# A fused attention, selective-scan and quantised-FFN kernel: silu groups moved to ScalarE, a fourth of eight products by C moved to VectorE, and a reordered front

## The reference

```
h = tok(x)                                   # patches, 12-head attention
h = concat([h, txt], axis=1)
h = h + mixer(layernorm(h))
h = h + ffn(layernorm(h))

mixer:  xi, res = split(x @ W_in)            # 384 channels each
        u = silu(causal_conv4(xi) + conv_b)
        delta, B, C = split(u @ W_x, [48, 64])
        delta = softplus(delta @ W_dt + b_dt)
        a = exp(cumulated later delta * A)   # A = -exp(A_log), 384 x 16
        xs = cumsum(delta*u*B * a) / (a + 1e-12)
        y = sum over the 16 states of xs * C, plus u * D
        return (y * silu(res)) @ W_out
ffn:    bitlinear (ternary weights, 8-bit activations), silu(gate)*up, bitlinear
```

## Time and profile before

| | before |
|---|---|
| runs, median | 541.2 us (537.76 to 542.29) |
| profiled execution, its own time | 541.64 us |
| its span | 539.8 us |
| front, up to the first scan | 139.8 us |
| first scan to the end of the last guarded states | 139.8 to 503.7 us |
| tail | 503.7 to 539.8 us |
| mean granted TensorE clock | 0.855 |

### The profile page before, as it was taken

One profiled execution on the slowest core, in us unless ns is written; L12 is line 12 of the kernel. 1 busy time (PEld: TensorE's weight loads), 2 busy tenths in 40 slices (PEclk: granted clock), 3 DMA queues, 4 the chain that ended last, 5 costly groups with the idle time before them and its releaser, 6 DMA issues.

```text
span 539.8 us, 5082 instructions
## 1 busy us (share of the span) xinstructions
PE 397.8 (74%) x1484; PEld 222.7 (41%) x1484; DVE 399.8 (74%) x481; ACT 338.3 (63%) x601; POOL 367.3 (68%) x288
## 2 busy tenths in 40 slices
PE   5929999686896585899677599875656686665753
PEld 1303677353553242565343356542323352332523
DVE  3024255622589899989999988989999989879544
ACT  1102544413967876777779857996886786796253
POOL 3002563002878988979998998998789999969401
PEclk9968999968798887999678889998987887778865
DMA  8390000005600003710000470000056100000000
GB/s 314 83 205 10 1 2 0 2 0 185 286 0 5 1 1 128 279 60 4 0 1 17 159 273 21 4 22 0 0 177 231 60 2 22 1 1 0 0 23 22
DMA packets 11547, 35.10 MB, mean 65 GB/s; under 512 B 2320, under 2 KB 6208, under 8 KB 11296
## 3 DMA queue, kind: packets, MB, share of 16 engines
q1 hardware_dynamic: 11120, 33.99, 18.7%
q10 hardware_dynamic: 400, 0.79, 0.4%
HBM read 33.40 MB, written 1.38 MB: 64 GB/s over the span
## 4 chain that ended last, share of the span: by engine, by line
POOL 31%; DVE 11%; PE 9%; issue 9%; ACT 6%; DVEq 0%; ACTq 0%; POOLq 0%
POOL big L465 15%; POOL big L471 10%; DVE PS L1305 5%; PE PS L817 4%; PE PS L593 3%; POOL big L509 2%; ACT PS L1001 2%; DVE big L1314 1%; PE PS L743 1%; DVE big L1320 1%; POOL big L447 1%; DVE big L1399 1%; ACT big L1053 1%; ACT big L1010 1%; PE PS L797 1%
## 5 line engine op out<-in xcount | busy, mean ns | idle before, releaser
L817 PE MATMUL PS<-big,eighth 128*128 128x384 f32 x384 | 170.9, 583 | 74.3 <-POOL big L471 73.2
L1305 DVE TENSOR_TENSOR_SCAN PS<-PS,big 128x768 f32<-128x768 f32 x96 | 168.6, 1756 | 18.5 <-ACT PS L1001 16.2
L465 POOL TENSOR_TENSOR big<-big,bc 128x768 f32<-128x768 f32 x96 | 175.1, 1839 | 0.0
L817 PEld LDWEIGHTS PS<-big,eighth 128*128 128x128 f32 x384 | 81.9, 224 | 144.8 <-POOL big L471 93.6
L471 POOL TENSOR_TENSOR big<-big,bc 128x768 f32<-128x768 f32 x60 | 109.5, 1824 | 37.3 <-DVE big L1314 37.1
L1001 ACT ACTIVATE PS<-big,Aneg 128x384 f32<-128x384 f32 x192 | 103.7, 572 | 39.6 <-DVE big L1320 25.4
L1010 ACT ACTIVATE big<-big,guard,Ahalf 128x380 f32<-128x380 f32 x192 | 122.5, 690 | 0.0
L1314 DVE SCALAR_TENSOR_TENSOR big<-big,PS 128x768 f32<-128x768 f32 x60 | 57.0, 951 | 5.8 <-ACT big L1010 0.5
L430 POOL TENSOR_TENSOR big<-bc,cst_sb 96x1536 f32<-96x1536 f32 x8 | 22.0, 2753 | 56.2 <-ACT bc L911 45.9
L593 PE MATMUL PS<-big,w_in_sb 96*128 96x384 f32 x96 | 42.9, 586 | 5.5 <-DVE big L1266 5.0
L593 PE MATMUL PS<-big 128*64 128x34 f32 (+3 forms) x400 | 43.8, 287 | 0.0
(11 more groups left out here) (152 smaller groups left out, 486.8 us busy)
## 6 DMA issues: line engine op xcount, KB each, us to landing
bc<-bc_rows SPq DMA_DIRECT2D x32, 768.0 KB, 4.4
bc<-in_x_cols_dram SPq DMA_DIRECT2D x3, 512.0 KB, 6.5
bc<-in_x_cols_dram SPq DMA_DIRECT2D x1, 1536.0 KB, 8.7
out_dram<-h SPq DMA_DIRECT2D x4, 288.0 KB, 2.3
big<-in_f_in_dram SPq DMA_DIRECT2D x1, 768.0 KB, 18.0
bc<-in_cw_dram ACTq DMA_DIRECT2D x1, 576.0 KB, 5.7
h<-in_bo_dram SPq DMA_DIRECT2D x3, 192.0 KB, 15.1
w_in_sb<-in_w_in_dram SPq DMA_DIRECT2D x1, 576.0 KB, 13.0
```

The lines of the kernel that those rows point to most:

```text
L465: P.tensor_tensor(pair(vR[:, g % VRING]), part(du, q, m).unsqueeze(1).broadcast_to([128, PAIR, QT]), rows_of(g, 0), ALU.mult).then_inc(sem ...
L817: ins = pe.matmul(y_sum, eighth[:, :], vR[:, g % VRING, QT * e:QT * (e + 1)], start=False, stop=True, skip_group_check=True)
L1305: V.tensor_tensor_scan(h_, h_, vR[:, g % VRING], 0.0, ALU.mult, ALU.add).then_inc(sem("scan_done"), 1)
```

## The change

Four things are changed together.

1. Silu of u and z becomes one ACT instruction from PSUM each, three in a row (`su`, `sz`), two steps or more after the matmuls they read. The DVE multiplications go. The factor 2 and the halves that made up for it go too.
2. DVE multiplies by C at four of eight pairs in place of three; in group 3 at pairs 1, 3, 4 and 7.
3. The preparation of group 1 no longer has six steps ahead of step 0; all of it stands beside steps 0 to 21. Small ACT instructions on a spare tile (`warm`) are put in so that a table is loaded ahead of its first use: softplus, Exp, and Silu in the tail.
4. The two FFN weight loads stand ahead of the nine loads of the bias and the text. Each group's output is stored in two parts.

```diff
-VECTOR_C = (1, 4, 6)
+VECTOR_C = ((1, 3, 4, 6), (1, 3, 4, 6), (1, 3, 4, 6), (1, 3, 4, 7))
...
-             cv0=-26, cv1=-25, cv2=-24, tu0=-25, tu1=-24, tu2=-23, us0=-24, us1=-23, us2=-22, x=-21, x_out=-20,
-             dt0=-19, dt1=-19, dt2=-19, sp=-18, times_u=-16, later0=-14, later1=-11, later2=-9, edges=-6,
-             z0=-16, z1=-15, z2=-14, tz0=-15, tz1=-14, tz2=-13, zs0=-14, zs1=-13, zs2=-12)
+             cv0=-26, cv1=-25, cv2=-24, su=-22, x=-18, x_out=-17,
+             dt0=-16, dt1=-16, dt2=-16, sp=-15, times_u=-13, later0=-14, later1=-12, later2=-9, edges=-6,
+             z0=-14, z1=-13, z2=-13, sz=-11)
...
-FIRST_MIXER = dict(stats=-6, root=-6, xn=-5, turn=-5, turned=-4, xi0=-3, xi1=-2, xi2=-2, tap0=0, tap1=0, tap2=1,
-                   cv0=1, cv1=2, cv2=2, tu0=2, tu1=3, tu2=3, us0=4, us1=5, us2=5, x=6, x_out=7, dt0=8, dt1=8, dt2=8, sp=9,
-                   times_u=11, later0=12, later1=14, later2=17, edges=19, z0=12, z1=13, z2=14, tz0=13, tz1=14, tz2=15,
-                   zs0=14, zs1=15, zs2=16)
+FIRST_MIXER = dict(stats=0, root=1, xn=2, turn=2, turned=3, xi0=3, xi1=4, xi2=4, tap0=4, tap1=5, tap2=5,
+                   cv0=5, cv1=6, cv2=6, su=8, x=13, x_out=14, dt0=15, dt1=15, dt2=15, sp=16,
+                   times_u=18, later0=17, later1=18, later2=19, edges=21, z0=11, z1=12, z2=12, sz=14)
...
-FIRST_STEP, LAST_STEP = -6, STEPS + 33
+FIRST_STEP, LAST_STEP = 0, STEPS + 33
...
-SCALAR_WORK = dict(xn=3, turned=2, tap0=1, tap1=1, tap2=1, tu0=1, tu1=1, tu2=1, tz0=1, tz1=1, tz2=1, x_out=1, sp=6,
+SCALAR_WORK = dict(xn=3, turned=2, tap0=1, tap1=1, tap2=1, su=5, sz=5, x_out=1, sp=6,
...
+            load("ffn", f_in_raw, f_in.rearrange("p m n -> p (m n)"))
+            load("ffn", f_out_raw, f_out.rearrange("p m n -> p (m n)"))
...
-            load("ffn", f_in_raw, f_in.rearrange("p m n -> p (m n)"))
-            load("ffn", f_out_raw, f_out.rearrange("p m n -> p (m n)"))
...
-            def store(q):
-                sp.wait_ge(sem("left_f2"), ORDINAL["f2", q, 1])
-                sp.dma_start(out[QB * q:QB * (q + 1)].rearrange("b l d -> (b l) d").rearrange("(i p) d -> p i d", p=128),
-                             tiles(q)).then_inc(sem("out_stored"), 16)
+            def store(q, j):
+                sp.wait_ge(sem("left_f2"), ORDINAL["f2", q, j])
+                t = slice(2, 3) if j else slice(0, 2)
+                sp.dma_start(out[QB * q:QB * (q + 1)].rearrange("b l d -> (b l) d").rearrange("(i p) d -> p i d", p=128)[:, t],
+                             tiles(q, t)).then_inc(sem("out_stored"), 16)
...
-            def tanh_z(q, j):
+            def silu_z(q, j):
...
-                A.activation(part(sres, q, j), job_bank("z", q, j)[:, 0:QT], ACT.Tanh, scale=0.5).then_inc(sem("tz_ready"), 1)
-            def tanh_first():
+                A.activation(part(sres, q, j), job_bank("z", q, j)[:, 0:QT], ACT.Silu).then_inc(sem("left_z"), 1)
+            def silu_u(q, j):
+                job_here(act, "cv", q, j)
+                if q >= 2:
+                    act.wait_ge(sem("y_acc"), QSTEPS * (q - 2) + BLOCK * j + 1)
+                    act.wait_ge(sem("du_ready"), delta_of(q - 2, j))
+                A.activation(part(u, q, j), job_bank("cv", q, j)[:, 0:QT], ACT.Silu).then_inc(sem("left_cv"), 1)
+            def silu_first():
...
-                A.activation(part(du, 0), part(u, 0), ACT.Tanh, scale=0.5).then_inc(sem("tu_first"), 1)
+                A.activation(part(u, 0), part(u, 0), ACT.Silu).then_inc(sem("u_first"), 1)
...
-                A.activation(xdbc[:, :], job_bank("x", q, 0)[0:F, 0:QT], ACT.Identity, scale=0.5).then_inc(sem("left_x"), 1)
+                A.activation(xdbc[:, :], job_bank("x", q, 0)[0:F, 0:QT], ACT.Copy).then_inc(sem("left_x"), 1)
...
-                for j in range(CT):
-                    for q in due("tu%d" % j, g):
-                        tanh_u(q, j)
-                for j in range(CT):
-                    for q in due("tz%d" % j, g):
-                        tanh_z(q, j)
+                for q in due("su", g):
+                    for j in range(CT):
+                        silu_u(q, j)
+                for q in due("sz", g):
+                    for j in range(CT):
+                        silu_z(q, j)
...
+                for q in due("center", g):
+                    if q == LAST:
+                        A.activation(warm[:, 2:3], v128[:, 0:1], ACT.Silu)
...
                 if i == 8:
-                    tanh_first()
+                    silu_first()
+                    silu_z(0, 0)
+                    silu_z(0, 1)
                 p = i - 1
...
                 if i == 9:
+                    A.activation(warm[:, 0:1], v128[:, 0:1], ACT.Softplus)
                     x_out(0)
...
                     first_tap(0, 2)
-                    tanh_z(0, 0)
                 if i == 8:
-                    tanh_z(0, 1)
-                    tanh_z(0, 2)
+                    silu_z(0, 2)
             for m in range(CT):
                 softplus(0, m)
+            A.activation(warm[:, 1:2], v128[:, 0:1], ACT.Exp)
             for g in range(FIRST_STEP, 0):
...
-                V.tensor_scalar(diagD[:, m, :], ident, dpar[:, m:m + 1], 0.25, ALU.mult, ALU.mult)
-            V.tensor_scalar(eighth[:, :], ident, 0.125, None, ALU.mult)
+                V.tensor_scalar(diagD[:, m, :], ident, dpar[:, m:m + 1], None, ALU.mult)
+            V.tensor_scalar(half_eye[:, :], ident, 0.5, None, ALU.mult)
...
-            def silu_z(q, j):
-                job_here(dve, "z", q, j)
-                dve.wait_ge(sem("tz_ready"), CT * q + j + 1)
-                V.scalar_tensor_tensor(part(sres, q, j), part(sres, q, j), 1.0, job_bank("z", q, j)[:, 0:QT],
-                                       ALU.add, ALU.mult).then_inc(sem("left_z"), 1)
-            def silu_first():
...
                     conv(0, 2)
-                    silu_z(0, 0)
-                if i == 8:
-                    silu_first()
-                    silu_z(0, 1)
-                    silu_z(0, 2)
             V.memset(gR.rearrange("p s (r l) -> p (s r) l", l=L)[:, :, L - 1:L], 1.0).then_inc(sem("edges_set"), 1)
```

More of the change, by code:

```diff
@@ L119 @@
 for i in range(NTL):
-    LAST_READ.update({"xi%d" % i: "tap%d" % i, "cv%d" % i: "us%d" % i, "z%d" % i: "zs%d" % i, "dt%d" % i: "sp", "out%d" % i: "add%d" % i,
+    LAST_READ.update({"xi%d" % i: "tap%d" % i, "cv%d" % i: "su", "z%d" % i: "sz", "dt%d" % i: "sp", "out%d" % i: "add%d" % i,
                       "gate%d" % i: "silu", "up%d" % i: "times%d" % i})
@@ L400, in _ @@
                 if q >= 2:
-                    store(q - 2)
-            store(2)
-            store(3)
-            sp.wait_ge(sem("out_stored"), 16 * NQ)
+                    store(q - 2, 0)
+                    store(q - 2, 1)
+            for q in range(NQ - 2, NQ):
+                store(q, 0)
+                store(q, 1)
+            sp.wait_ge(sem("out_stored"), 32 * NQ)
         @block.gpsimd
@@ L816, in sum_y @@
                 for e in range(PAIR):
[L817 removed]
+                    ins = pe.matmul(y_sum, half_eye[:, :], vR[:, g % VRING, QT * e:QT * (e + 1)], start=False, stop=True,
                                     skip_group_check=True)
@@ L1429, in after @@
                         gate(q, m)
-                for j in range(CT):
-                    for q in due("us%d" % j, g):
-                        silu_u(q, j)
-                for j in range(CT):
-                    for q in due("zs%d" % j, g):
-                        silu_z(q, j)
                 for j in range(2):
```

17 lines of the change are left out of this document (3 added, 14 removed).

## The result

The change makes the kernel faster: 517.76 us median of four runs (515.52 to 523.06) against 540.92 of the kernel before on the same chip, ratio 0.959 with a 95% interval of 0.951 to 0.968. The forecast was 516, range 507 to 527.

What follows compares the result with a forecast made beforehand. No engine full over the whole span; DVE 93% full in the steps, POOL close behind. From 541.64: loads -12.8, front's end -8.4, DVE's work +3.0, DVE's waits -5.3, tail -1.9, giving 516.2 us; 80% range 507 to 527.

Steps and rivals of the forecast that it cites:

- Loads, -12.8: Front: FFN weights land sooner, PE's 10.7 us wait and 2.1 us of half clock go; -12.8 us, bounds -9.3 and -12.8.
- The rival that the weights don't land sooner: Front: the images, not small pieces, hold the queue, so the 12.8 us is not gained; 529 us, chance 0.07.
- End of the front, -8.4: Front's end: projection's wait, softplus table and group 1's preparation no longer delay the first scan; -8.4 us, bounds -5 and -8.4.
- DVE's work, +3.0: Steps: 12 products by C add 11.5 us, norm statistics 1.2; z and u multiplications drop 4.9 and 4.8; net +3.0.
- DVE's waits, -5.3: Steps: DVE's waits become 11.2 us in place of 16.5, six new ACT blocks costing 1.0 each; -5.3 us.
- Tail, -1.9: Tail: the last product by C leaves POOL, so the tail begins 1.9 us sooner for PE; -1.9 us.
- What would show it: Expected trace signs: gapless PE, first scan near 118.5, DVE over 94%, POOL under 87%, ACT waits about 11 us.
- three marks against me: Wrong if scans behind new blocks wait over 2.5 us, first scan passes 122, or DVE's POOL/PE waits exceed 4 us.
- Expensive blocks: Steps: each new ACT block costs DVE the worst-case 2.48 us; 525 us, chance 0.15.
- DVE bound to the full: Steps: ACT's blocks hide and DVE waits only where it did for ACT; 507 us, chance 0.10.
- ACT becomes the bound: Steps: each of six blocks is exposed whole, 30.6 us in all, and the old 16.5 stay; 552 us, chance 0.03.
- A switch that stops ACT twice as long: Steps: a table switch stops ACT 2.56 us, a block takes 6.6 us; 532 us, chance 0.03.

Runs made afterwards that it cites:

- second profile: The changed kernel run again with no edit and profiled anew: span 517.1 us, profiled execution 518.9 us, median 517.98 us, ratio 0.958.
- silu as before: Kernel before with the change's loads, front order, tables ahead and four-of-eight products, but single Tanh and DVE multiplications kept, projection at step 10: 519.32 us, 0.965.
- first profile: The changed kernel's original profiled execution, the slowest of its four runs: 523.06 us, span 521.3 us.
- two more moves: Changed kernel, group 1's z behind its projection, group 3's at step 69, group 2's at 28 to 31, group 1's convolutions spread: 510.42 us, 0.941.
- four of eight alone: Kernel before with one edit, DVE multiplying by C at four of eight pairs: 538.69 us, ratio 0.997.
- run without switches: Changed kernel with Tanh in place of Silu in the six blocks of groups 1 to 3, so no table switch: 508.72 us, 0.947.

## Why the prediction was right, and which of its steps were not

The sum was 516.2; the second profile has 518.9, the median is 517.8. By the stretches of the table (the last product by C, 0.96 us, lies behind the last scan) it foresaw -21.2 in the front, -3.3 in the steps and -0.9 in the tail. Measured on the second profile: -23.1, +1.7, -1.4. Errors of 1.9 and 5.0 us of opposite sign met in the sum, so the time was nearer than its parts: that much of the hit is luck.

- *Loads, -12.8.* Right in mechanism and a little small: 14.4 us to the first scan. The wait of 10.7 went whole and the half clock did not come back, which gave 2.3 (16.80 us in place of 19.13), put at 2.1. Another 0.6 is that PE was through with the patch embedding at 29.16 in place of 29.80, which lies within the spread told below as open; the last 0.8 was not traced. The rival that the weights don't land sooner is out.
- *End of the front, -8.4.* 8.7 (125.4 to 116.7). The 2.2 of the projection's wait is right: 2.25 us, gone here and back in silu as before. But the wait ended with the multiplication of z, which the bank hung on, and not with that of u, and the projection behind it ran at a granted clock of 0.58 there, 3.60 us in place of 2.10. These 1.5 us the working did not have. The rest came with the order of group 1's preparation, by the rows alone: no run put that order back. That the table ahead gains nothing of its own stood in the working (the third softplus waits for PE), and the run without it shows it.
- *DVE's work, +3.0.* +2.6 up to the last scan, where 2.0 of the 3.0 were due. The terms were not all there: the running sums, which I took as constant, moved with POOL.
- *DVE's waits, -5.3.* This is the step that failed. Idle fell by 0.9 (26.7 to 25.7), or not at all in the first profile. By the terms, in the second profile:
  - The waits for POOL, 2.3, for PE's FFN output, 2.0, and for Tanh, 0.7, went as counted.
  - The 2.8 for PE's sums, put down to POOL's lag and counted as gone, stayed at 2.9. Of the old ones 0.6 was left at step 25, but the moved convolutions of group 1 brought a new one of 2.3 at step 9 (it goes in two more moves, where they are spread).
  - Of the 8.7 on ACT's account 1.1 stayed, away from the new blocks, where I had left 5.2. I laid this to Tanh's place next to the convolution; four of eight alone took 4.4 off with Tanh where it was, so that reason is not shown.
  - The six new blocks, put at 1.0 each, are the term that missed most: DVE's waits behind the three of z were 3.5, 3.4 and 4.6 us (3.8, 3.4 and 4.6 in the first profile), and nearly nothing behind the three of u. That is 11.5 in all against 6.0. The run without switches gives the same from the other side, 10.9 us of idle.

  So errors of +2.9, -4.1 and +5.5 make up nearly all of the 4.4 us by which the step was off. The average of the nine old waits was no measure, since a block costs by what stands next to it: z of groups 2 and 3 has the FFN's block two steps on, z of group 1 a bank that PE hands over. I had named both places and allowed under 3 us for the bank; the stop was 2.79 and the scan's wait 3.81.
- *Tail, -1.9.* -1.4 by the stretch, where -0.9 was due, once the projection has the same clock. In the profiled execution PE's half clock in the output projection took 2.6 us of it back; nothing in the working allowed for that.
- *What would show it* (numbers of the first profile). PE without a gap, at full clock: yes. First scan near 118.5: 116.2. POOL under 87%: 84% (306.85 of 364.34). DVE over 94%: no, 92.6% (337.34). Waits on ACT about 11: 13.0 without the one ahead of the first scan. Waits on POOL gone: yes, and those on PE 3.6, under the 4 that I had set. Of the three marks against me one was met: two scans behind new blocks waited over 2.5 us, 3.81 and 2.73.
- *Rivals.* "Expensive blocks" came half true: its two places are where the waits are, and their 11.8 us (first profile) lie between the 6.0 of the forecast and its 14.9. "DVE bound to the full", 507, did not come; the run without switches, 508.7, shows about what it would have given. "ACT becomes the bound" is out: it had 30.6 us of new waits. A switch that stops ACT twice as long is out: in the rows above Silu follows its load by 0.01 us, and decays follow theirs by as little. The Trainium skill's drain of about 1380 ns per switch, "ScalarE: Activation LUTs", section "What ACT_TABLE_LOAD costs", does not show in this kernel; its 1283 ns do.

What stays open: the first scan of kernels with the same front lay between 114.4 and 116.7. Most of this is there when PE comes to the product of the sums, at 28.5 in the soonest of them and 30.2 in the latest; from there to the first scan it is 85.9 to 86.5 us in all. Why the patch embedding ahead of it ends sooner in some was not followed up.

## What to carry to other kernels

A switch of ACT's table is paid where ACT's lead is short, so the price of such a block is read from the steps next to it, not from the mean of others. Moving two of the blocks, one away from a buffer that another engine waits for and one from two steps ahead of the FFN's block to six behind it, made the silu groups worth 8 us where nothing could be told of them before. Two further moves, of a third block and of the convolutions, gained nothing: their waits went too, but others came. A load on which a relay of engines hangs goes to the head of its queue, ahead of small pieces that nobody needs yet: that was 13 us for two moved lines. And when work moves between DVE and POOL, the rest of both must be priced anew, since some of their instructions hold each other up.
